# Interleaving GpSimd's two split chains, with a remainder buffer for each

## The reference

```python
x = x + _L0_attn_ref(_layernorm(x), ...)           # 16 heads of 8, 4 key/value heads
x = x + _L0_xattn_ref(_layernorm(x), ctx, ctx, ...)  # 16 heads of 8
x = x + _L0_ffn_ref(_layernorm(x), ...)            # 8 experts, 2 for a token, a shared one
x = x + _L1_attn_ref(_layernorm(x), ...)           # 4 shared heads of 64, relative bias
x = x + _L1_xattn_ref(_layernorm(x), ctx, ctx, mask, ...)  # 16 heads of 8, masked
x = x + _L1_ffn_ref(_layernorm(x), ...)
```

```python
Q, K, V = x @ Wq.T + bq, y @ Wk.T + bk, y @ Wv.T + bv
attn = softmax(einsum('blhd,bmhd->bhlm', Q, K) * scale)
out = einsum('bhlm,bmhd->blhd', attn, V) @ Wo.T + bo
```

## Time and profile before

| what | value |
| --- | --- |
| runs, us | 1085.68, 1090.24 (median), 1093.18 |
| span of the profiled execution, us | 1087.7 |
| PE busy | 973.1 us, 89% |
| DVE busy | 855.0 us, 79% |
| ACT busy | 692.1 us, 64% |
| POOL busy | 649.3 us, 60% |
| HBM | 107 GB/s over the span |

### The profile page before, as it was taken

How to read it: one execution, slowest core, us unless ns; L and a number is a source line. 1 busy time by engine, 2 the same in 40 slices (tenths; PEclk the granted TensorE clock), 3 DMA queues, 4 the chain that set the end, 5 groups by cost and what they waited for, 6 DMA issues and landing times.

```text
span 1087.7 us, 33962 instructions
## 1 busy us (share of the span) xinstructions
PE 973.1 (89%) x10494; PEld 694.1 (64%) x10494; DVE 855.0 (79%) x2398; ACT 692.1 (64%) x1801; POOL 649.3 (60%) x1020
## 2 busy tenths in 40 slices
PE   3699999989998888999998889889999999768997
PEld 2466666656665667777776677665656655556885
DVE  6588899888888778888887888776787877657665
ACT  1377777777776743555665887673666666546775
POOL 8757778877676466640675786168667752323443
PEclk9599999999998979999998999998999999989999
DMA  5776567985666201332332111035555640054551
GB/s 147 181 148 132 116 139 163 185 162 134 143 153 171 74 34 50 98 105 77 106 104 55 37 31 38 26 64 133 115 113 129 130 106 18 6 196 167 194 193 29
DMA packets 81460, 119.69 MB, mean 110 GB/s; under 512 B 16720, under 2 KB 62704, under 8 KB 80288
## 3 DMA queue, kind: packets, MB, share of 16 engines
q1 hardware_dynamic: 66704, 85.24, 32.9%
q0 software_dynamic: 9472, 27.27, 8.2%
q10 hardware_dynamic: 5136, 5.31, 2.5%
HBM read 80.75 MB, written 36.18 MB: 107 GB/s over the span
## 4 chain that ended last, share of the span: by engine, by line
PE 61%; DVE 19%; issue 8%; DMA 5%; ACT 3%; POOL 3%; SPq 1%; DVEq 0%; POOLq 0%; ACTq 0%
PE heads_ps_pv L992 4%; PE heads_ps_max L970 4%; DVE heads_neg_max L770 4%; PE cross_ps_max L960 4%; PE experts_ps_gu L2488 4%; PE cross_ps_max L970 3%; PE cross_ps_pv L992 3%; DMA QK<-heads_qk_parts 2%; PE experts_ps_gu L2490 2%; PE experts_ps_gu L2489 2%; PE heads_ps_out L1054 2%; PE experts_ps_y L2509 2%; PE experts_ps_y L2510 2%; PE experts_ps_hT L2496 1%; PE cross_ps_qk L1316 1%
## 5 line engine op out<-in xcount | busy, mean ns | idle before, releaser
L770 DVE TENSOR_REDUCE heads_neg_max<-heads_ps_max 128x4 f32<-128x512 f32 x256 | 169.5, 681 | 36.0 <-PE heads_ps_max L970 34.4
L844 ACT ACTIVATE heads_E<-heads_ps_exp 128x512 f32<-128x512 f32 x256 | 150.1, 603 | 22.1 <-PE heads_ps_pv L992 17.3
L970 PE MATMUL heads_ps_max<-QK 48*128 48x128 bf16 x1024 | 102.9, 226 | 10.2 <-DMA QK<-heads_qk_parts 5.8
L770 DVE TENSOR_REDUCE cross_neg_max<-cross_ps_max 128x4 f32<-128x512 f32 x128 | 86.2, 682 | 29.5 <-PE cross_ps_max L970 28.9
L974 PE MATMUL heads_ps_exp<-QK 50*128 50x128 bf16 x1024 | 103.0, 222 | 0.0
L2182 POOL DMA_INDIRECT experts_gathered<-experts_y_dram,experts_index x64 | 62.0, 969 | 65.4 <-DMA experts_y_dram<-experts_y_sb 44.1
L844 ACT ACTIVATE cross_E<-cross_ps_exp 128x512 f32<-128x512 f32 x128 | 76.5, 599 | 33.1 <-PE cross_ps_exp L974 17.0
L2404 ACT ACTIVATE experts_act_out<-experts_ps_gu 128x256 f32<-128x256 f32 x110 | 42.3, 384 | 83.0 <-PE experts_ps_gu L2490 82.9
L970 PEld LDWEIGHTS heads_ps_max<-QK 48*128 48x128 bf16 x1024 | 58.9, 97 | 52.2 <-issue 21.0
L1613 POOL TENSOR_TENSOR experts_hidden_lo<-experts_hidden,experts_hidden_hi 128x512 fp32r<-128x512 f32 x32 | 41.4, 1293 | 73.9 <-ACT experts_hidden_hi L1837 66.8
L992 PE MATMUL heads_ps_pv<-heads_E,heads_V 128*32 128x128 f32 x2048 | 84.8, 285 | 0.0
(11 more groups left out here) (325 smaller groups left out, 3173.3 us busy)
## 6 DMA issues: line engine op xcount, KB each, us to landing
experts_share<-experts_cT_dram SPq DMA_DIRECT2D x7, 2304.0 KB, 8.8
heads_qk_parts<-heads_parts POOLq DMA_DIRECT2D x32, 384.0 KB, 4.7
QK<-heads_qk_parts SPq DMA_DIRECT2D x64, 192.0 KB
QK<-heads_qk_parts SPq DMA_DIRECT2D x64, 128.0 KB
cross_qk_parts<-cross_parts POOLq DMA_DIRECT2D x16, 384.0 KB, 4.2
QK<-cross_qk_parts SPq DMA_DIRECT2D x32, 192.0 KB
experts_xs_dram<-load_stats SPq DMA_DIRECT2D x26, 192.0 KB, 3.0
experts_xs<-experts_xs_dram SPq DMA_DIRECT2D x78, 64.0 KB
```

The lines of the kernel that those rows point to most:

```text
L770: nc.vector.tensor_reduce(neg_max[:, half, heads.start:heads.stop], ps_max[:, u % 2, :].rearrange("q (h k) -> q h k", h=HU), AX.X, ALU.max ...
L844: nc.scalar.activation(E[:, half, heads.start:heads.stop, :], ps_exp[:, u % 2, :].rearrange("k (h q) -> k h q", h=HU), ACT.Exp, scale=scal ...
L970: last_max = nc.tensor.matmul(ps_max[:, u % 2, i * S:(i + 1) * S], QK[q_of][rows, 0, h, max_of], QK[q_of][rows, 1, h, max_of], start=not m ...
```

## The change

In `split` the chains of q and k no longer follow each other but alternate: q's cast, k's cast, q's remainder, k's remainder, q's second cast, k's second cast, q's last part, k's last part. Each instruction waits for the one two places before it, and no longer for its predecessor. The wait for k's projection moves ahead of k's first cast, the second instruction. So that both remainders can live side by side, `rest` becomes two buffers. When masked, k's chain goes first and the mask multiply of q stands ahead of both. A last wait for all instructions stays ahead of the store.

```diff
-        rest = sb("rest", [D, GT])
+        rest = [sb(f"rest_{c}", [D, GT]) for c in "qk"]
...
+            def split_done(t, n):
+                pool.wait_ge(split_step, t.group(SPLITS, FA * SPLITS + n))
+                apart(pool, t, turns_pool)
+            def projected(t, n):
+                pool.wait_ge(qk_ready, t.group(2, FA * 2 + n))
+                apart(pool, t, turns_pool)
...
-                for c in range(2):
-                    pool.wait_ge(qk_ready, t.group(2, FA * 2 + c + 1))
-                    apart(pool, t, turns_pool)
-                    full = qk_full[:, c, :]
-                    hi, mid, lo = (made[:, c, r if c == 0 else PARTS - 1 - r] for r in range(PARTS))
-                    def did(ins):
-                        nonlocal a
-                        a += 1
-                        ins.then_inc(split_step, 1)
-                        pool.wait_ge(split_step, t.group(SPLITS, FA * SPLITS + a))
-                        apart(pool, t, turns_pool)
-                    if masked and c == 0:
-                        did(nc.gpsimd.tensor_tensor(qm[:]..., full..., any_all[:]..., ALU.mult))
-                        full = qm[:]
-                    did(nc.gpsimd.tensor_scalar(hi, full, 1.0, 0.0, ALU.mult, ALU.add))
-                    did(nc.gpsimd.tensor_tensor(rest[:], full, hi, ALU.subtract))
-                    did(nc.gpsimd.tensor_scalar(mid, rest[:], 1.0, 0.0, ALU.mult, ALU.add))
-                    did(nc.gpsimd.tensor_tensor(lo, rest[:], mid, ALU.subtract))
+                m = 1 if masked else 0
+                projected(t, 1)
+                if masked:
+                    nc.gpsimd.tensor_tensor(qm[:]..., q_full..., any_all[:]..., ALU.mult).then_inc(split_step, 1)
+                    projected(t, 2)
+                    (full0, rest0, parts0), (full1, rest1, parts1) = (k_full, rest[1][:], k_parts), (qm[:], rest[0][:], q_parts)
+                else:
+                    (full0, rest0, parts0), (full1, rest1, parts1) = (q_full, rest[0][:], q_parts), (k_full, rest[1][:], k_parts)
+                nc.gpsimd.tensor_scalar(parts0[0], full0, 1.0, 0.0, ALU.mult, ALU.add).then_inc(split_step, 1)
+                if masked:
+                    split_done(t, 1)
+                else:
+                    projected(t, 2)
+                nc.gpsimd.tensor_scalar(parts1[0], full1, 1.0, 0.0, ALU.mult, ALU.add).then_inc(split_step, 1)
+                split_done(t, m + 1)
+                nc.gpsimd.tensor_tensor(rest0, full0, parts0[0], ALU.subtract).then_inc(split_step, 1)
+                split_done(t, m + 2)
+                nc.gpsimd.tensor_tensor(rest1, full1, parts1[0], ALU.subtract).then_inc(split_step, 1)
+                split_done(t, m + 3)
+                nc.gpsimd.tensor_scalar(parts0[1], rest0, 1.0, 0.0, ALU.mult, ALU.add).then_inc(split_step, 1)
+                split_done(t, m + 4)
+                nc.gpsimd.tensor_scalar(parts1[1], rest1, 1.0, 0.0, ALU.mult, ALU.add).then_inc(split_step, 1)
+                split_done(t, m + 5)
+                nc.gpsimd.tensor_tensor(parts0[2], rest0, parts0[1], ALU.subtract).then_inc(split_step, 1)
+                split_done(t, m + 6)
+                nc.gpsimd.tensor_tensor(parts1[2], rest1, parts1[1], ALU.subtract).then_inc(split_step, 1)
+                split_done(t, m + 8)
```

7 lines of the change are left out of this document (4 added, 3 removed).

## The result

The changed kernel takes 1125.26 us (median of 4 runs, 1119.37 to 1126.99); the kernel before, run beside it, 1091.71 (4 runs). The ratio is 1.0307 with a 95% interval of 1.0263 to 1.0352: slower by 3%, and outside the predicted range, which ended at 1105. The profiled execution of the changed kernel took 1119.37 us with a span of 1117.5, that is 29.8 more than the span before.

A forecast was written before the change was run, and what follows sets the result against it. It took the kernel to be bound by PE and DVE, with GpSimd delaying DVE's shift pair. Terms -2.5 + 1.2 + 3.2 + 1.9 = +3.8 us gave 1094.0 on the median, range 1081 to 1105.

The forecast's parts named there:

- the even step outside the loops: Shift pair gets in behind the bias add, ending 6.27 against 6.16: +0.11 us a group, +1.2 over 11 groups.
- Start: First three groups' splits lose their gaps and the transfers follow: -2.5 us, bounds -0.9 and -2.7; third store near 33.8.
- The split: GpSimd's eight casts and subtractions run without gaps, about 4.05 us; store before at 5.29 outside the loops, 6.46 inside.
- Odd steps outside the loops: DVE meets the split: cast over at 0.81, subtract at 1.48 (+0.29), normalisations at about 2.5 (+0.54 us).
- Loops: 16 groups: even pair ends 5.82 if on time, 6.65 behind the bias add; midway +0.2 each, +3.2, bounds -3.2 and +9.6.
- Masked stage: 11 groups: odd shift meets the casts, +0.25 us, a third covered by PE: 0.17 each, +1.9, bounds 0 and +2.8.
- PE's wait: PE said to sit idle 32.7 us before the matmul turning the softmax shift (L1035), waiting for DVE's L800.
- Rival 2: Even pair always just late for the gap between store and bias add, deciding at 5.64 us: +15.4, 1105.6 us; chance 0.2.
- Rival 3: Only the start gains; losses at the port shared by DVE and GpSimd move but cancel: 1087.7 us; chance 0.2.
- Rival 1: DVE's odd shift cast slips in ahead of k's cast, odd steps get faster: -9.4, 1080.8 us; chance 0.2.
- Rival 4: GpSimd without gaps keeps DVE out until the split is over: +3.2 us in 38 groups, +121, 1211 us; chance 0.02.

The follow-up runs named there:

- experiment 7: Kernel before with the second remainder buffer alone, old order and old waits; 1097.12 us, ratio 1.0015.
- experiment 6: Changed kernel with L249 alone held back outside the loops until DVE has written the even shift; 1114.82 us, ratio 1.0204.
- experiment 11: Changed kernel with L249 waiting for the bias add ahead of it outside the loops, a gap of about 0.08 us; 1102.59 us, one run.
- experiment 1: Changed kernel with the bias add, from step 4 on, waiting until DVE has written the even shift; 1099.03 us, ratio 1.0104.
- experiment 12: Changed kernel with each split instruction waiting for its predecessor again, and L249 waiting for the bias add outside the loops; 1096.83 us, ratio 1.0076.
- experiment 4: Changed kernel with the bias add held for the even shift and the split paused after two casts for the odd shift; 1105.40 us, ratio 1.0139.
- experiment 8: Interleaved split only before step 4 of each call, the old chains from there on; 1096.66 us, ratio 1.0003 to the kernel before.
- experiment 3: Changed kernel with each L249 cut into two instructions of half the columns; 1122.92 us, ratio 1.0283.
- experiment 13: Changed kernel with L249 outside the loops waiting on the previous group's bias add, a wait already met; 1124.25 us, ratio 1.0262.
- experiment 14: Changed kernel with L249 moved ahead of the bias add outside the loops, directly behind the store; 1115.11 us, one run.
- experiment 10: Changed kernel with one more GpSimd subtraction right behind the bias add in the loops, result unused; 1117.11 us, one run.
- experiment 5: Changed kernel with the bias add held for the even shift and the split held until both normalised tiles are written; 1101.03 us, ratio 1.0076.

## Why the prediction was wrong

**The step that failed** is the even step outside the loops: "L704 runs 5.28 to 6.02 and lets go at 5.88; L798 then 5.88 to 6.05, L800 6.09 to 6.27". Everything up to it is in the trace, in most of the eight groups: the cast arrives at 5.73 (predicted 5.77), the bias add runs 5.28 to 6.02. But nothing was let in at 5.88. I had used the kernel before to exclude that DVE is kept out by instructions without a gap (store to L704), and carried this over to the next pair, L704 to L249. That pair stands in the timeline of the kernel before right behind the L704 of the earlier trace rows, with an overlap of 0.05 us:

```profile
203.37 1.28 POOL L249 TENSOR_TENSOR experts_gate_up_lo<-experts_whole,experts_gate_up_hi 128x512 fp32r<-128x512 f32 x1
```

In that trace no shift came in between, so it could not show what happens then; experiment 7 has one. Nor is the opening behind the store firm: in the changed kernel's first loop the same pair, store and bias add, lets the cast in in six groups and keeps it out in one (93.67). My upper bound for this step, +0.5 us a group, contained no case in which the pair sits out L249 as well; the measured delay is 7.70 - 6.10 = 1.60 on average, or 12.8 us over the eight groups. Experiments 6 and 11 show the cause: with L249 held back, or with a gap of 0.08 us ahead of it, the stretch loses nothing.

**What was missing from the sum** is the clock. The prediction has no term for it. Of the 18.55 us, 12.8 would be the delay itself if each group paid it in full; the other 6 fit the 22 us at half clock behind waits of 1.17 to 1.99 us, and both vanish together in experiments 1, 6, 11 and 12. That the idle time alone does it, whoever causes it, experiment 4 makes likely (a transfer late by 1.8 us, then 0.50); no run changed the clock by itself, so the split of the 18.55 is argued, not shown.

**The terms one by one.**

- Start: predicted -2.5, third store near 33.8; measured -2.77, at 33.54. The working was right for the store. That the transfers behind it follow, with nothing else in the way, was not: 0.83 us is left where the third load lands, 1.85 at the ninth store, and in experiment 8, where nothing else differs, 0.22. Five other traces with the changed kernel's code up to there (3, 6, 11, 13, 14) have the ninth store between 0.87 us earlier and 0.15 later. The lower bound of -0.9 was the better number. The sum has no term for what the gapless split does to DVE's normalisations in the start (experiment 8).
- The split: predicted 4.05 us without gaps in and out of the loops; measured 4.05 (187.11 to 191.16). Right.
- Odd steps outside the loops: predicted cast over at 0.81, subtract at 1.48, normalisations at 2.5; measured 0.81, 1.44, 2.49. Right, and by experiment 1 of no consequence.
- Loops: predicted +0.2 a group between "on time" (5.82) and "behind L704" (6.65). Measured 6.45 to 6.73 in all groups of the first loop; +11.3 us over the 15 group intervals, 0.75 each, above even the bound of 0.6. Experiment 1 shows it to be the bias add: without it in front, +2.0. I had averaged the two cases, but the first fails by itself. In most groups the cast is on time, at 5.38 in the lines above (first cast at 109.68). The store lets it in at 5.53, not at the 5.43 of the working; so its subtract comes at 5.74, and the bias add has begun at 5.68. In experiment 1, with the bias add held back, the same cast is in at 5.45.
- Masked stage: predicted +1.9; +4.92, of which 1.62 in the four steady groups at its end, 0.4 each in place of 0.17. I had priced the odd step alone; the even pair, over at 6.06 before in groups 44 to 47, is now over at 6.25 to 6.75.
- PE's wait: the 32.7 us of the earlier trace rows were read as time in which PE sat idle. They are the sum of two rows of the profile; the matmuls waited 11.2 us. No term of the sum used the figure.

**The rivals.** Rival 2, the bias add in the way, was right for the loops by its mechanism and its price (+9.6 against 11.3); its mark of 5.64 us is passed by the subtract, in most groups not by the cast. It did not see L249. Rival 3 fails as a whole, and experiment 8 shows no gain of the start alone that can be measured. Rival 1 did not happen: the odd subtract takes 0.60 us outside the loops. Rival 4, no opening at all, was given 0.02 and priced at 1211; outside the loops it does not hold inside the split, where DVE gets in between instructions that overlap by 0.03 us (187.74 and 187.95 above). But it is just what happens at L722 and L249, and in the start it happens inside the split too (experiment 8).

**What stays open.** Why DVE is shut out each time at bias add and L249, and elsewhere only at times (store and bias add at 93.67, the split of the start, bias add and the added instruction at 267.65). Its length alone is not it (experiment 3: 256 columns behind the bias add keep DVE out; in the masked stage of the changed kernel an L249 of 256 or 128 columns, also without a gap, lets the cast in three times of three), though between the halves of experiment 3 the cast got in ahead of 256 columns and not ahead of 384. That an instruction without a gap follows is not enough (experiments 10 and 14), nor a wait in between (13). No run changed where its operands lie, or its kind. None of the variants was shown to be faster than the kernel before; of those with the interleaved order everywhere, experiments 5 and 12 come nearest, both at 1.0076 with intervals just above 1; that of experiment 1 (1.0104) includes 1.

## What to carry to other kernels

When two engines shut each other out, shortening one's sequence moves everything behind it: list what now stands where the other engine's urgent instruction arrives, down to the second instruction behind, and price the wait through all of them. A row that shows one opening is evidence for that pair of instructions at most. If a small urgent instruction must get in, let the long one wait for a signal that is not yet there (experiments 1, 6 and 11), since a wait already met leaves no gap (experiment 13); and where PE is near its limit, price a wait of over a microsecond with the stretch at half clock that came behind five such waits of eight here.

## What the runs showed of the hardware

- Two GpSimd instructions whose records overlap by 0.02 to 0.06 us let a waiting DVE instruction in between most pairs (inside the split, bias add to L296, L249 to bias add), and not between the bias add and L249 outside the loops: 8 groups of 8 in the changed kernel, 8 of 8 with L249 halved, 8 of 8 with a wait that was met. Pairs that let it in as a rule kept it out at times, in the start through most of the split (35.20 in experiment 8). The Trainium skill (SBUF — State Buffer, section SBUF: two separate sides) says that of a DVE instruction in a 2-port mode or with two SBUF inputs and a GpSimd instruction the one that starts first has the shared port pair for the whole instruction and the other blocks; the cast of 1.56 us shows a block through two instructions in a row.
- A gap of 0.08 us ahead of L249 was enough for two DVE instructions, not one (190.05 in experiment 11, started with L249's record and over in 0.17).
- PE's granted clock was 0.50 for some 3 to 7 us behind single idle times of 1.17 to 1.99 us, whether DVE (207.72 in the changed kernel) or a transfer (experiment 4) caused them; behind three idle times of 1.16 to 1.18 us it stayed at 1.00.
